# A Householder step with fewer waits on VectorE, another order on TensorE and ScalarE, and a shorter scalar program on GpSimd

## The reference, cut to what matters

```
h = max(layernorm(x), 0)
deg = A.sum(0) + A.sum(1) - diag(A);  d = rsqrt(deg)
_, U = eigh(d[:,None] * (diag(deg) - A) * d[None,:])
x = x + U @ (relu((U.T @ h) @ W1 + b1) @ W2 + b2)
h = max(layernorm(x), 0)
x = x + gnn_lstm(h, adj, ...)      # two convolutions, LSTMs over windows of 1 to 4 nodes
```

## Time and profile before

| what | value |
|---|---|
| time, median of 3 runs | 1301.23 us (1301.19 to 1301.62) |
| profiled execution, its own time | 1300.82 us |
| span of that execution | 1298.8 us |
| TensorE busy | 1216.6 us, 94% |
| VectorE busy | 936.8 us, 72% |
| ScalarE busy | 912.0 us, 70% |
| GpSimd busy | 335.6 us, 26% |
| granted TensorE clock, mean | 0.978 of full |

### The profile page before, as it was taken

The page is one execution under the profiler, slowest core; times in us unless marked ns, Lnnn a source line. Parts: engine busy times, 40 slices in busy tenths (PEclk is TensorE's granted clock), DMA queues, the critical chain, the costliest instruction groups (busy, mean ns, idle before and its releaser), DMA issues.

```text
span 1298.8 us, 26438 instructions
## 1 busy us (share of the span) xinstructions
PE 1216.6 (94%) x7973; PEld 1072.9 (83%) x7973; DVE 936.8 (72%) x4624; ACT 912.0 (70%) x3309; POOL 335.6 (26%) x1206
## 2 busy tenths in 40 slices
PE   9999999997662799999999999999999999999997
PEld 7777888875652688889889889899899899899897
DVE  8999999999999777757755655645645645655655
ACT  5777888886993022479479578578578578587676
POOL 0388888888888200000300000000000000000000
PEclk9999999997997799999999999999999999999999
DMA  9600000000000033000100100100100100000001
GB/s 265 142 2 2 2 2 2 2 2 1 1 1 1 1 98 98 1 1 2 33 0 0 32 0 0 33 0 0 32 0 3 29 0 16 16 0 16 17 1 33
DMA packets 43631, 28.86 MB, mean 22 GB/s; under 512 B 1520, under 2 KB 39440, under 8 KB 43536
## 3 DMA queue, kind: packets, MB, share of 16 engines
q1 hardware_dynamic: 43536, 27.81, 7.8%
HBM read 19.42 MB, written 8.39 MB: 21 GB/s over the span
## 4 chain that ended last, share of the span: by engine, by line
PE 76%; DVE 19%; ACT 3%; issue 1%; DMA 1%; ACTq 0%; DVEq 0%; SPq 0%
PE bank L943 15%; PE bank L933 11%; PE bank L938 9%; PE bank L946 8%; PE bank L717 4%; PE bank L739 3%; PE bank L728 3%; PE bank L863 2%; PE bank L915 2%; PE bank L907 2%; PE bank L871 2%; PE bank L726 2%; PE bank L901 2%; PE bank L878 2%; PE bank L886 2%; PE bank L733 2%
## 5 line engine op out<-in xcount | busy, mean ns | idle before, releaser
L654 ACT ACTIVATE BIG<-bank,bias 128x128 f32<-128x128 f32 (+2 forms) x544 | 226.7, 417 | 161.6 <-PE bank L946 102.1
L943 PE MATMUL bank<-spare,wT 128*128 128x256 f32 (+2 forms) x1408 | 311.5, 321 | 0.0
L654 ACT ACTIVATE PV<-bank,bias 128x256 f32<-128x256 f32 (+2 forms) x704 | 301.6, 431 | 0.0
L943 PEld LDWEIGHTS bank<-spare,wT 128*128 128x128 f32 x1408 | 234.8, 191 | 13.2
L933 PE MATMUL bank<-spare,wT 128*128 128x128 f32 (+2 forms) x1088 | 226.4, 319 | 4.1 <-DVE spare L1665 2.7
L1651 DVE TENSOR_TENSOR BIG<-BIG,PV 128x128 f32<-128x128 f32 (+2 forms) x192 | 62.9, 328 | 207.6 <-ACT BIG L654 207.6
L933 PEld LDWEIGHTS bank<-spare,wT 128*128 128x128 f32 x1088 | 169.5, 191 | 19.2 <-DVE spare L1665 6.1
L946 PE MATMUL bank<-spare,wT 128*128 128x128 f32 (+2 forms) x768 | 169.7, 303 | 0.0
L938 PE MATMUL bank<-spare,wT 128*128 128x128 f32 (+2 forms) x768 | 141.7, 307 | 3.6 <-DVE spare L1663 1.2
L662 ACT ACTIVATE spare<-spare 128x256 f32<-128x256 f32 (+2 forms) x352 | 133.1, 378 | 4.2 <-DVE spare L1654 3.9
L946 PEld LDWEIGHTS bank<-spare,wT 128*128 128x128 f32 x768 | 125.2, 191 | 3.3
(11 more groups left out here) (495 smaller groups left out, 2738.7 us busy)
## 6 DMA issues: line engine op xcount, KB each, us to landing
spare<-in_x SPq DMA_DIRECT2D x32, 256.0 KB, 4.0
out<-X SPq DMA_DIRECT2D x32, 256.0 KB, 2.4
spare<-in_L_gnn_Wih SPq DMA_DIRECT2D x4, 256.0 KB, 4.9
spare<-in_L_gnn_Whh SPq DMA_DIRECT2D x4, 256.0 KB, 4.1
W<-in_L_gnn_W SPq DMA_DIRECT2D x2, 64.0 KB, 2.8
Wg<-in_L_gnn_Wg SPq DMA_DIRECT2D x2, 64.0 KB, 2.5
adj<-in_adj SPq DMA_DIRECT2D x1, 64.0 KB, 1.8
X<-in_x SPq DMA_DIRECT2D x4, 0.5 KB, 17.2
```

The source lines that it names most:

```text
L654: last = nc.scalar.activation(gate_out[q][i][:, 0:T], gate(i, q, T), ACT.Tanh if q == GATE_G else ACT.Sigmoid, bias=bias[:, at:at + 1])
L943: last = nc.tensor.matmul(gate(i, q, T), wT[:, 0, p - 1, q * D:(q + 1) * D], xt, start=True, stop=(j == 0))
```

## The change

- **VectorE**: `XA` is gone; `HX` is one operation, XM * alpha * eta, behind `AM`. `AM` raises `ya_in`, `V_` raises `a_in`. The dot product, `YA` and the second update of `A` now each wait for one joint semaphore (`uy_in`, `ya_in`, `a_in`) that both producers raise, in place of two or three waits.
- **TensorE**: the row product of `x` is 256 columns wide (`base[:, 0:2 * N]` into bank 0; the right half is read by nobody); the negative row stands behind y's two products and has no wait of its own; `IDLE_BEHIND` is 128 in place of 256.
- **ScalarE**: `eta_row` stands between the two statistics in place of ahead of both.
- **GpSimd**: each sweep has two picking products in place of three and no memset (one memset stands ahead of the loop), four memsets stand ahead of the wait for `leaf_ready`, and the sign factors stand ahead of the last sweep in place of behind it.

```diff
-IDLE_BEHIND = 256
+IDLE_BEHIND = 128
 ...
-MINUS_S, ETA, HV_STEP = 2, 5, 15
+MINUS_S, ETA, HV_STEP = 2, 5, 12
 ... ScalarE, step k
-    nc.scalar.activation(u_row(k)[:, t + 1:N], banks[0][:, t + 1:N], ACT.Copy).then_inc(taken, 1)
+    nc.scalar.activation(u_row(k)[:, t + 1:N], banks[0][:, t + 1:N], ACT.Copy).then_inc(uy_in, 1)
 ...
+statistic(2 * k)
 if t + 1 < N:
     act.wait_ge(xb_ready, 2 * k + 2)
     act.wait_ge(hv, at_hv(k, ETA))
     nc.scalar.activation(eta_row[:, t + 1:N], banks[3][:, t + 1:N], ACT.Copy,
-                         scale=eta[:, t:t + 1]).then_inc(taken, 1)
-statistic(2 * k)
+                         scale=eta[:, t:t + 1]).then_inc(a_in, 1)
 statistic(2 * k + 1)
 ... TensorE, householder(k)
-    nc.tensor.matmul(banks[0][:, 0:N], x_wide, ident[:, 0:N], start=True, stop=True).then_inc(xb_ready, 1)
-    if k:
-        pe.wait_ge(taken, taken_by(k - 1, ETA_ROW))
+    nc.tensor.matmul(banks[0][:, 0:2 * N], x_wide, base[:, 0:2 * N], start=True, stop=True).then_inc(xb_ready, 1)
+pe.wait_ge(a_ready, k + 1)
+nc.tensor.matmul(banks[2][:, from_t], x_wide, A[:, from_t], start=True, stop=True).then_inc(uy_in, 1)
+if t + 1 < N:
+    nc.tensor.matmul(banks[4][:, 0:1], A[:], x_c, start=True, stop=True).then_inc(ya_in, 1)
     nc.tensor.matmul(banks[3][:, 0:N], x_wide, minus_ident[:], start=True, stop=True).then_inc(xb_ready, 1)
-pe.wait_ge(a_ready, k + 1)
-nc.tensor.matmul(banks[2][:, from_t], x_wide, A[:, from_t], start=True, stop=True).then_inc(yrow_ready, 1)
-if t + 1 < N:
-    nc.tensor.matmul(banks[4][:, 0:1], A[:], x_c, start=True, stop=True).then_inc(ycol_ready, 1)
 ... VectorE, reflector(k)
     dve.wait_ge(hv, n_al)
-    n_xa = step(V.tensor_tensor(S(XA), S(XM), alpha[:, t:t + 1], ALU.mult))
-    n_am = step(V.tensor_tensor(S(AM), below[:, t:t + 1], alpha[:, t:t + 1], ALU.mult))
-    dve.wait_ge(hv, n_xa)
-    n_hx = step(V.tensor_tensor(S(HX), S(XA), eta[:, t:t + 1], ALU.mult))
-    dve.wait_ge(hv, n_am)
-    dve.wait_ge(taken, taken_by(k, ROW))
-dve.wait_ge(yrow_ready, k + 2)
+    V.tensor_tensor(S(AM), below[:, t:t + 1], alpha[:, t:t + 1], ALU.mult).then_inc(ya_in, 1)
+    dve.wait_ge(hv, n_eta)
+    step(V.scalar_tensor_tensor(out=S(HX), in0=S(XM), scalar=alpha[:, t:t + 1], in1=eta[:, t:t + 1],
+                                op0=ALU.mult, op1=ALU.mult))
+dve.wait_ge(uy_in, 2 * k + (1 if last else 2))
 ...
-dve.wait_ge(ycol_ready, k + 1)
+dve.wait_ge(ya_in, 2 * k + 2)
 ... VectorE, update(k)
-n_v = step(V.scalar_tensor_tensor(out=S(V_), in0=S(HX), scalar=S(Z_), in1=S(W_),
-                                  op0=ALU.mult, op1=ALU.add))
+V.scalar_tensor_tensor(out=S(V_), in0=S(HX), scalar=S(Z_), in1=S(W_),
+                       op0=ALU.mult, op1=ALU.add).then_inc(a_in, 1)
 below_of(t)
-dve.wait_ge(taken, taken_by(k, ETA_ROW))
-dve.wait_ge(hv, n_v)
+dve.wait_ge(a_in, 2 * k + 2)
 ... GpSimd, one sweep
-for c, v in enumerate((d16[:, 1:16], d16[:, 0:15], e16[:, 0:15])):
-    go(TT(pick[:, c, 0:15], v, oh[:, 0:15], ALU.mult))
-op(nc.gpsimd.memset(pick[:, :, 15:16], 0.0))
+go(TT(pick[:, 0, 0:15], d16[:, 1:16], oh[:, 0:15], ALU.mult))
+op(TT(pick[:, 1:3, 0:15], d_and_e[:, :, 0:15], oh[:, 0:15].unsqueeze(1).to_broadcast([1, 2, 15]), ALU.mult))
 ... GpSimd, ahead of the last sweep (the 15 operations are as before)
+if k == QR_SWEEPS - 1:
+    factors()
```

More of the change, by code:

```diff
@@ L166, in build @@
         s_ready = sem("s_ready")
-        yrow_ready = sem("yrow_ready")
-        ycol_ready = sem("ycol_ready")
+        corner = sem("corner")
+        uy_in = sem("uy_in")
+        ya_in = sem("ya_in")
+        a_in = sem("a_in")
         taken = sem("taken")
@@ L202, in build @@
         eta_row, minus_ident = m[0], UT
-        ROW, COL_U, COLUMN, ETA_ROW = range(1, 5)
+        COL_U, COLUMN = range(1, 3)
         def taken_by(k, what):
-            return 1 + 4 * k + what
-        MINUS_S, ETA, HV_STEP = 2, 5, 15
+            return 1 + 2 * k + what
+        MINUS_S, ETA, HV_STEP = 2, 5, 12
         def at_hv(k, what):
@@ L228, in build @@
         d16, e16 = leaf[LP, 0:16], leaf[LP, 16:32]
+        d_and_e = leaf[LP, 0:32].rearrange("p (c f) -> p c f", f=LEAF)
         am = leaf[LP, 32:48]
@@ L369, in _ @@
                 op(TT(pick[:, :, 0:w], pick[:, :, 0:w], pick[:, :, w:2 * w], ALU.add))
+            op(nc.gpsimd.memset(pick[:, :, 15:16], 0.0))
             go(TT(SIG, SIG, SIG, ALU.mult))
@@ L377, in _, with L, factors @@
             op(TS(d16, d16, SE, 1.0, ALU.mult, ALU.mult))
+            def L(i, n=1):
+                return sc[:, i:i + n]
+            def factors():
+                pool.wait_ge(rs_in, 3)
+                op(TT(L(ZZ, 3), L(ZZ, 3), L(INV + 1, 3), ALU.mult))
+                go(TS(L(LINKED), L(ZZ), L(43), None, ALU.is_gt))
+                go(TS(L(CC, 3), L(CC, 3), 0.0, None, ALU.is_lt))
+                go(TS(L(LF), V4[:, 0, 0:1], 0.0, None, ALU.is_gt))
+                op(TS(L(LF + 1), V4[:, 0, 0:1], 0.0, None, ALU.is_lt))
+                op(TS(L(ZZ, 3), L(ZZ, 3), L(43), None, ALU.is_le))
+                for l in (2, 1, 0):
+                    op(TS(L(LF, 2), L(LF, 2), L(CC + l), L(ZZ + l), ALU.subtract, ALU.mult))
+                    op(TS(L(LF, 2), L(LF, 2), 1.0, L(CC + l), ALU.mult, ALU.add))
+                go(TT(L(LFA), L(LF), L(LF + 1), ALU.add))
+                nc.gpsimd.tensor_tensor(L(LFB), L(LF), L(LF + 1), ALU.subtract).then_inc(rs_out, 1)
+                q.last(pool)
+                nc.gpsimd.tensor_scalar(L(LFA), L(LFA), -1.0, None, ALU.add).then_inc(rs_out, 1)
             for k in range(QR_SWEEPS):
+                if k == QR_SWEEPS - 1:
+                    factors()
                 go(TT(y16[:, 0:15], d16[:, 0:15], d16[:, 1:16], ALU.mult))
@@ L464, in _ @@
             TS(S(PAR), T0, 1.0, S(PAR), ALU.add, ALU.mult).then_inc(leaf_sign, 1)
[L466 to L478, removed]
-            go(TT(L(LFA), L(LF), L(LF + 1), ALU.add))
-            nc.gpsimd.tensor_tensor(L(LFB), L(LF), L(LF + 1), ALU.subtract).then_inc(rs_out, 1)
-            q.last(pool)
-            nc.gpsimd.tensor_scalar(L(LFA), L(LFA), -1.0, None, ALU.add).then_inc(rs_out, 1)
             pool.wait_ge(ln_var, 3)
```

8 lines of the change are left out of this document (4 added, 4 removed).

## The result

The changed kernel takes 1287.17 us (median of 4 runs, 1286.81 to 1288.18) against 1301.42 us (median of 4, 1301.19 to 1301.8) of the kernel before: a ratio of 0.989, 95% interval 0.9878 to 0.9903. The forecast was 1291.3 with a range of 1286.5 to 1298.0. The profiled execution took 1288.18 us, with a span of 1286.4; it is the slowest of the four, and the other three are 0.8 to 1.4 us shorter.

What follows compares the result with a forecast made beforehand. The 127 serial Householder steps bound it: early by long updates of A, late by VectorE's scalar chain. 2.4 + 4.4 + 3.4 - 0.3 = 9.9 us off 1300.8, plus 0.4 for the median, gives 1291.3 us; range 1286.5 to 1298.

Steps and rivals of the forecast that it cites:

- Waits on VectorE: Dot product and second update of A: joint semaphores save 0.07 us each, 0.15 for a dot product behind a late product.
- both rivals about waits: VectorE: waits cost nothing, only operations count (1299.7 us, 13%); joint semaphore saves only 0.07 behind late product too (1295.5, 15%).
- HX: VectorE, late step: HX in one operation lets the dot product start at 251.41 in place of 251.50.
- the chain of 2.02: VectorE's own chain through the scalars in the late step, put at 2.11 - 0.09 = 2.02 us.
- The new limit of the late steps: Late steps: the wide row product delays ScalarE's copy, then ACOL, which W_ needs; floor of 2.08 us a step.
- The late term: 75 late Householder steps: mean 2.12 us against 2.165, 0.045 a step, 3.4 us saved.
- the allowance of 0.03 for single long steps: Middle and late steps: 0.03 us added to the mean for single long steps, not expected to go away.
- Early and middle: 14 early steps at 2.17 us, 2.4 us saved; 34 middle steps at 2.14, 4.4 us saved.
- The trim: TensorE's last product shortened: costed at nothing; without it TensorE would be late for the next x.
- GpSimd: Sweeps and sign factors behind the stage: off the path, VectorE and GpSimd shift alike, 3.1 us to spare.
- The 0.3 for step 0: Step 0: eta_row now stands behind the first statistic, which waits for the input's DMA; 0.3 us lost once.
- steps of 2.5 us, all 127: Householder stage, clock rival: TensorE's clock falls, all 127 steps slow, 1335 us; chance 4%, say 1305 us.

Runs made afterwards that it cites:

- e7: The kernel before with the joint semaphores alone, HX still in two operations and GpSimd's old program: 1292.86 us, ratio 0.9937.
- e5: The changed kernel with each producer on its own semaphore again, the rest of the change kept: 1297.71 us, ratio 0.9971 to before.
- e6: The kernel before with HX in one operation and nothing else of the change: 1296.42 us, ratio 0.9962.
- e9: The changed kernel with TensorE's and ScalarE's order of before, row product 128 columns wide, 256 idle columns: 1285.46 us, ratio 0.988 to before.
- e12: As e9 but with 128 idle columns, sign factors still ahead of the last sweep: 1287.33 us, ratio 0.9893 to before.
- e2: The kernel before with the changed GpSimd program only: 1300.08 us, ratio 0.9993.
- e11: The changed kernel with 256 idle columns in place of 128, wide row product kept: 1301.05 us, ratio 0.9998 to before.
- e3: The changed kernel with the sign factors behind the last sweep again, the shorter sweeps kept: 1286.64 us, ratio 0.9889 to before.

## Why the prediction was right, and where it was not

**Waits on VectorE: right.** Priced at 0.07 where nothing else is late and 0.15 behind a late product, they measured 0.07 (`XM` to the second update, 0.19 to 0.12; in e7 also `HX` to the dot product, 0.15 to 0.08) and 0.14 (0.18 to 0.04). e5 and e7 show that it is the semaphores and nothing else of the change. This settles both rivals about waits. The count that matters is not quite that of the `wait_ge` calls: the dot product's two further waits were one instruction in the queue (50 ns), and cost together what the update's single one did (21 ns) where nothing was late. The Trainium skill's rule against it ("VectorE: DVE Perf Modes", "Rules for kernel authors": fewer operations, not fewer semaphores) is not borne out here: fewer waits gave 13.6 us alone, one operation fewer 4.0.

**`HX`: right in kind.** Nothing early; its late gain of 0.049 a step alone (e6) shrinks to 0.013 beside the joint semaphores (e9 against e7). Where `A` is 20 columns wide and less, the chain of 2.02 came out at 2.03 to 2.06.

**The new limit of the late steps: wrong.** "This is the new limit of the late steps: 2.08", said of `ACOL`, failed. The columns' price was right (0.21) and so was the copy's start (1.22; measured 1.22 to 1.23), but `ACOL` follows the copy by 0.36 to 0.38, not by the 0.42 of the earlier trace rows, which came from a step where ScalarE's `UC` between them stood behind `minus_s` (it started at 250.96, 0.04 behind that one's end, and 0.13 behind the copy; here the distance is 0.08). The sum for `ACOL` is then 2.02 to 2.04, not 2.08. `ACOL` ends before `W_` wants it, by a hundredth of a microsecond more than the handover takes, and the chain through the scalars sets the step. I had worked that chain out and then set it aside for a sum with 0.04 to 0.06 of slack in it. e12 confirms it: an earlier copy did not shorten the late steps.

**The late term: mis-sized, 3.4 against 7.2 us.** The 3.8 us are 0.05 a step: 2.12 foreseen, 2.069 measured. About 0.02 of it is the limit above (2.08 against a median of 2.06), 0.02 the allowance of 0.03 for single long steps, which I did not expect to go away, and 0.01 the rounding up to 2.12. The long steps mostly did go: the mean of the late steps is 0.007 over their median, where it was 0.018. All four kernels with the waits apart (before, e2, e5, e6) have four to six late steps over 2.27, up to 2.54; those with joint semaphores have none, or one of 2.40 to 2.45, but for e11, which has three. Why separate waits should now and then cost 0.3 us was not tried.

**Early and middle: right** (2.17 and 2.14 foreseen; 2.178 and 2.130 measured), with p late as worked out (`Z_` at 0.145 foreseen, 0.17 measured): e9, where p has time, does an early step in 2.138.

**The trim: right, and larger than anything else.** "Without the trim TensorE would be late for the next x" was put down with no price. It is 14 us (e11): the whole gain. It only takes back what the wide row product added, though: e9, with neither the trim nor the wide product, is no slower.

**GpSimd: wrong.** "VectorE and GpSimd shift alike here" failed. The old last sweep began at 415.39, and the factors in its place at 415.93, though the stage around them had moved by 14.7 us. The sweeps did begin 3.3 us earlier (52.6 for 55.9), since step 15 ends earlier and four memsets stand ahead of the wait, and were 4.9 ahead at the eleventh (275.0 for 279.9). They lost all of it in the five sweeps from there to the factors, 140.9 us for 135.5, more of which now runs beside the second stage's VectorE work. To give were GpSimd's idle time ahead of the factors (425.07 - 415.39 = 9.7 us) and the 3.1 us in front of TensorE, 12.8 in all. By the forecast's 9.9 nothing would have been late; by the real 14.7, 1.9 us are, and 1.6 were lost. That these two agree is in part luck: GpSimd came 0.5 later than this has it, TensorE's product for the sign needs 0.5 of its own, and factors and sweep took 15.2 us (415.93 to 431.15), not the 16.8 foreseen.

So side and range held, the range not by much: 1287.17 is 0.7 above its lower end and just below the 1287.5 to 1294.5 given for the mechanism itself. Two errors of opposite sign helped. Against the profiled execution the forecast was 2.7 too high (1290.9 against 1288.18). The stage ended 4.8 us earlier than foreseen (14.7 against 9.9): 3.8 from the late term, 0.4 from the middle one, 0.1 less from the early one, 0.5 ahead of the first stretch (0.3 later foreseen, 0.2 earlier measured) and 0.1 between the first and the second. Of that GpSimd took 1.6, and the last stage, which the change leaves alone, 0.7 (851.4 us for 850.7); 0.2 came back outside the span. Against the median the forecast was 4.1 too high. The 0.3 for step 0 was about right by itself: its second `x` comes at 13.74 to 13.92 in the kernels with the new order and at 13.42 to 13.75 in those with the old order and joint semaphores.

One figure of the prediction does not follow from its own numbers: steps of 2.5 us, all 127, would add 0.29 to the mean step of 2.21, and give about 1337 us and not 1335, and by "0.35 to 0.4 over today's" it would be 1345 or more. The clock stayed at 1.00 in the stage, so nothing hangs on it.

## What to carry to other kernels

In a serial chain, count the waits in front of each instruction, and join the semaphores of producers that one reader needs: it costs no operation. When one engine's chain gets shorter, list every filler and every side program that was sized for the old length, and subtract the gain from its slack: here 128 idle columns kept beside a product made 128 columns wider would have cost 14 us, and a side program with 12.8 us of slack was late by the rest. An added limit is only real if each distance in it was measured between instructions that did not wait for something else.

## What the runs showed of the hardware

GpSimd's small operations became slower once VectorE had long ones beside them. The same operation in the changed kernel, in the Householder stage (60 to 260 us) and behind it (280 to 440), by groups of instructions (count, busy time, mean ns, idle before):

```profile
L453 POOL TENSOR_TENSOR leaf<-leaf 1x4 f32<-1x4 f32 x63 | 12.5, 198 | 4.2
```

```profile
L453 POOL TENSOR_TENSOR leaf<-leaf 1x4 f32<-1x4 f32 x35 | 10.8, 310 | 2.3
```

In the kernel before, the second mean was 208: its sweeps met other VectorE work. In e9 it is 263, in e12 307, and in e3 363, although e3's sweeps behind the stage were among the shortest of the kernels with the faster steps; so this one operation does not tell how long a sweep gets. The timeline of the changed kernel shows what happens:

```profile
290.74 1.23 DVE L1277 TENSOR_TENSOR PV<-BIG,PV 128x1024 f32<-128x1024 f32 x1
290.84 1.18 POOL L459 TENSOR_TENSOR leaf<-leaf 1x2 f32<-1x2 f32 x1
291.88 1.22 DVE L1278 TENSOR_TENSOR PV<-BIG,PV 128x1024 f32<-128x1024 f32 x1
292.09 1.06 POOL L453 TENSOR_TENSOR leaf<-leaf 1x4 f32<-1x4 f32 x1
```

Operations of 0.19 to 0.20 us on 2 and 4 numbers last until 0.05 us behind the end of VectorE's operation with two inputs in SBUF. Beside a reciprocal of 0.94 us, with one input, they do not:

```profile
428.90 0.94 DVE L1571 RECIPROCAL m<-m 128x128 f32<-128x128 f32 x1
429.15 0.55 POOL L430 TENSOR_TENSOR leaf<-leaf 1x1 f32<-1x1 f32 x1
```

L430 takes 0.55 (mean) in the Householder stage too. Of GpSimd's operations between 280 and 440 us that take at most 0.26 in the Householder stage, four start beside VectorE's additions of `BIG` and `PV` and take 1.12 (median), eight start beside a reciprocal of over 0.6 us on `m` and take 0.21. This agrees with the Trainium skill, "SBUF — State Buffer", section "Who interferes with whom": a VectorE instruction with two SBUF inputs contends with a GpSimd instruction that reads SBUF, one with at most one such input and outside the two-port modes does not. What it means for a program of this kind is that its length depends on which operations happen to meet: that e12's GpSimd came to the factors 3.8 us later than e9's fits this, but which meeting made the difference was not traced, and no experiment moved GpSimd's operations alone.
